# Order of small operations and a later GpSimd scaling in the norm between two attention layers

## The chip, the cores and the metric

The kernel runs on one core of a Trainium2 chip. The metric is the device time of one execution in microseconds. TensorE multiplies, VectorE and ScalarE read its results out of PSUM, GpSimd works on SBUF alone, SyncE (SP) issues the loads and stores.

## The reference, cut to what matters

Eight images of 512 channels by 32 x 32 pixels go through two attention layers. The change lies where the first ends and the second begins:

```python
# layer 0, for each image: x is (512, 1024)
out = w_proj @ a + b_proj                       # a: attention output
out = group_norm(out, gn2_scale, gn2_bias)      # 32 groups of 16 channels
x1  = x + out
# layer 1
qkv = w_qkv @ x1                                # rows of w_qkv normalised
rms = sqrt(mean(qkv ** 2, over channels)) + 1e-4
q, k, v = split(qkv / rms)
attn = softmax(q.T @ k * 512 ** -0.5)          # tokens by tokens, 1024 x 1024, one head
out  = (x1 + w_out @ (attn applied to v)) * 2 ** -0.5
```

## The kernel before

**Precision.** Each float32 matrix is held as two parts of the matmul type, hi (the value rounded) and lo (the rest), and a product is three matmuls: hi·hi, hi·lo, lo·hi. ScalarE writes the hi parts and VectorE the lo parts.

**Order of the work.** A loop runs over the eight images (batches); the code for each engine is a queue written out by hand, and the engines meet at semaphores. Two PSUM tiles of 128 x 1024, `big0` and `big1`, are used in turn by nearly every product; the list `BIG` gives the order. `released(key)` makes TensorE wait until the buffer's previous content (the key two places before in `BIG`) has been read. In the boundary the order is: projection tiles `proj` 0 to 3, Gram tiles `g` 0 to 3, then `y` 0 to 3.

**The boundary.** The 512 channels are four blocks of 128 (k = 0 to 3). Blocks 0 and 1 are normalised together as part c = 0 of the norm, blocks 2 and 3 as part c = 1. Part 1, on which the change bears, goes:

- VectorE: statistics of `proj` 2 and 3 (`out_stats`, L1222 to L1227), means (`gn2_mean`).
- TensorE: `gn2_means(1)`, two small matmuls that average over the channels of a group (L437, L439).
- VectorE: `gn2_dev(1)` squares the deviation of each channel's mean (L1096 to L1098).
- TensorE: `gn2_vars(1)`, two small matmuls that average the variances and the squared deviations (L444, L446).
- VectorE: `gn2_veps(1)` adds epsilon (L1101). GpSimd: `group_rstd` raises to -0.5 (L948). VectorE: `gn2_coefs(1)`, three small operations (L1105 to L1107).
- VectorE: `residual(2)` and `residual(3)` (L1252), which write `XA` = normalised out + x.
- ScalarE: `xc_hi` (L896), the hi part of x1. VectorE: `xc_lo` (L1257), its lo part. For blocks 0 and 1 the parts lie in `ST`, for blocks 2 and 3 in `HH` and `HL`.
- GpSimd: x1 itself in float32 (L1003), into `X`. It is read by `gram_product` and at the very end of layer 1.

**The Gram products.** The mean of the squares of q, k and v needs no product with all of w_qkv: with G = w_qkv^T w_qkv folded to its upper blocks, `from_x1` (L626) makes tile g k = the blocks j = 0 to k of G times x1, six matmuls a block (two halves of 512 columns by three parts). `gram_product(k)` on VectorE (L1263) multiplies that tile by float x1. GpSimd adds the four products (L1010), and TensorE sums them over channels (L668) between y 1 and y 2. y tile k (L626 too, 24 matmuls) needs the buffer of the Gram tile two places before it, so y 0 waits for product 2 and y 1 for product 3.

`x1_block(j)` makes TensorE wait for the lo part of block j. TensorE does what it can without blocks 2 and 3 first: tiles 2 and 3 from blocks 0 and 1, 24 matmuls in all, then block 2 of both tiles, then block 3 of tile 3.

**SP's queue** in this stretch: `W<-d_m` (weights of y) after the last projection tile; the next image into `XA` once all four x1 and all four lo parts are done; `W<-d_u` after the last Gram tile.

Of the kernel before, what the change touches and what calls it, by code (L numbers as in the profile page):

```python
# [20 lines left out]
KB = C // P  # L21
# [63 lines left out]
def build(nc, x, wv_t, wp_t, wqk_t, v_qkv, v_out, wo_t, vecs, consts, out):  # L85
    ctx = ExitStack()
    with ctx:
# [214 lines left out]
        def own_wait(eng):  # L302

            eng.sem_inc(s_waited, 1)
# [117 lines left out]
        def _(pe):  # L422
# [58 lines left out]
            def body(b, last_batch):  # L481
                def released(key):

                    i = big_at(b, key)
                    if i >= 2:
                        kind, k = (BIG_LAST if last_batch else BIG)[i - 2]
                        reader, per = {"v": (s_v_ready, 5), "qk": (s_nat_ready, 16), "s": (s_exp_done, 72),
                                       "proj": (s_pr_ready, 4), "gna": (s_gn_var, GN_PER_BATCH),
                                       "gnb": (s_gn_veps, GN_PER_BATCH),
                                       "g": (s_prod_ready, 4), "r": (s_r_ready, 1),  # L490
                                       "y": (s_y_ready, 4), "u": (s_vp_ready, 8), "s1": (s_s1_ready, 8)}[kind]

                        pe.wait_ge(reader, b * per + k + (GN_PER_BATCH if kind in ("gna", "gnb") else 1))

                    return big[i % 2]
# [108 lines left out]
                def gn2_vars(c):  # L604
                    group_vars(GN_PER_BATCH * b + 2 + c, tps[1][:, 0:2], slice(2 * c, 2 * c + 2), s_gn2_full)
# [15 lines left out]
                def from_x1(t, k, slot, blocks):  # L621
                    for half in range(2):
                        cols = slice(HALF * half, HALF * half + HALF)
                        for j in blocks:
                            for i, (wp, xp) in enumerate(((0, 0), (0, 1), (1, 0))):
                                last = mm(t[:, cols], w_full[slot][:, wp, j, P * k:P * k + P], x1(xp, j)[:, cols],  # L626
                                          start=(j == 0 and i == 0), stop=(j == (k if slot == 0 else KB - 1) and i == 2))
                    return last
# [14 lines left out]
                gn2_means(1)  # L643
                x1_block(1)
                from_x1(t, 1, 0, (1,)).then_inc(s_big_full, 1)
                g2 = released(("g", 2))
                from_x1(g2, 2, 0, (0,))
                gn2_vars(1)
                from_x1(g2, 2, 0, (1,))
                g3 = released(("g", 3))  # L650
                from_x1(g3, 3, 0, (0, 1))
                x1_block(2)
# [281 lines left out]
        @block.gpsimd  # L934
        def _(pool):
            nc.gpsimd.memset(expo[:, 0:8], 0.5)
            nc.gpsimd.memset(expo[:, 8:16], -0.5).then_inc(s_expo_set, 1)
            nc.gpsimd.memset(ones[:], 1.0)
            nc.gpsimd.memset(product_stage(2).bitcast(f32), 0.0).then_inc(s_const_set, 1)
            pool.wait_ge(s_expo_set, 1)  # L940
            for n, rows in ((4, slice(8, 12)), (12, slice(0, 8)), (16, slice(12, 16))):
                pool.wait_ge(s_square_sum, n)
                nc.gpsimd.tensor_tensor(rnorm[:, rows], ssq[:, rows], expo[:, 8:8 + rows.stop - rows.start], ALU.pow)\
                  .then_inc(s_norm_pow, 1)

            def group_rstd(n, rows):
                pool.wait_ge(s_gn_veps, n)
                nc.gpsimd.tensor_tensor(rstd[:, rows], veps[:, rows], expo[:, 8 + rows.start:8 + rows.stop], ALU.pow)\  # L948
                  .then_inc(s_gn_rstd, 1)

            group_rstd(1, slice(0, KB))

            def body(b, last_batch):
                def normalise(n):
                    i = n % 8
                    pool.wait_ge(s_recip_done, b * 72 + n + 1)
                    own_wait(pool)
                    nc.gpsimd.tensor_scalar(PB[:, i, :], PB[:, i, :], rinv[:, i:i + 1], 1.0, ALU.mult, ALU.mult)\  # L958
                      .then_inc(s_p_norm, 1)

                def head_out(u):
                    pool.wait_ge(s_corr_done, b * 16 + u + 1)

                    pool.wait_ge(s_p_norm, b * 72 + min(4 * u + 12, 4 * UNITS0))
                    if u == UNITS0 - 2:
                        pool.wait_ge(s_a_lo, b * 6 + 6)
                    rows, pair, c = slice(64 * (u // 2 % 2), 64 * (u // 2 % 2) + 64), u // 4, u % 2
                    nc.gpsimd.tensor_tensor(XA[rows, pair, HALF * c:HALF * c + HALF], RB[rows, 0:HALF],  # L968
                                            RB[rows, HALF:N], ALU.add).then_inc(s_a_done, 1)
                    pool.wait_ge(s_a_done, b * 16 + u + 1)  # L970
                    own_wait(pool)

                def scale_x(k):
                    if k == 0:
                        pool.wait_ge(s_x_res, b * 16 + 16)
                        own_wait(pool)
                    nc.gpsimd.tensor_scalar(X[:, k, :], X[:, k, :], RES, 1.0, ALU.mult, ALU.mult)\
                      .then_inc(s_x_scaled, 1)

                def a_lo(pair, half):  # L980
                    pool.wait_ge(s_a_hi, b * 8 + 2 * pair + half + 1)
                    cols = slice(HALF * half, HALF * half + HALF)
                    nc.gpsimd.tensor_tensor(HL[:, pair, cols], XA[:, pair, cols], HH[:, pair, cols].bitcast(f32),
                                            ALU.subtract).then_inc(s_a_lo, 1)

                for n in range(4 * UNITS0):
                    normalise(n)
                    if n % 4 == 3 and n >= 8:
                        head_out(n // 4 - 2)
                    if n in X_SCALE_STEPS:  # L990
                        scale_x(X_SCALE_STEPS.index(n))
                    for part in a_parts(n):
                        a_lo(*part)
                head_out(UNITS0 - 2)
                head_out(UNITS0 - 1)
                for c in range(GN2_PARTS):
                    rows = slice(2 * c, 2 * c + 2)
                    group_rstd(GN_PER_BATCH * b + 2 + c, rows)
                    pool.wait_ge(s_coef_b, b * GN2_PARTS + c + 1)
                    for k in (2 * c, 2 * c + 1):  # L1000
                        pool.wait_ge(s_res_sum, b * KB + k + 1)
                        own_wait(pool)
                        nc.gpsimd.tensor_scalar(X[:, k, :], XA[:, k, :], 1.0, coefB[:, k:k + 1], ALU.mult, ALU.add)\  # L1003
                          .then_inc(s_xc_ready, 1)
                for k in range(1, KB):
                    pool.wait_ge(s_prod_ready, b * KB + k + 1)
                    if k > 1:
                        pool.wait_ge(s_prod_add, b * (KB - 2) + k - 1)
                    own_wait(pool)
                    nc.gpsimd.tensor_tensor(PB[:, 4, :], PB[:, 4, :], PB[:, 4 + k, :], ALU.add)\  # L1010
                      .then_inc(s_prod_add if k < KB - 1 else s_prod_sum, 1)
                pool.wait_ge(s_ms_done, b + 1)
                nc.gpsimd.tensor_tensor(rms, mean_sq, expo[:, 0:8], ALU.pow).then_inc(s_rms_done, 1)
                for i in range(8):
                    if i == 4:
                        normalise(64 + 3)
                    pool.wait_ge(s_s1_ready, b * 8 + i + 1)
                    own_wait(pool)
                    nc.gpsimd.tensor_scalar(negmax[:, i:i + 1], rowmax1[:, i:i + 1], rcol[:, i:i + 1], -1.0,  # L1019
                                            ALU.mult, ALU.mult).then_inc(s_neg_ready, 1)  # L1020
                    if i == 7 and not last_batch:
                        group_rstd(GN_PER_BATCH * (b + 1) + 1, slice(0, KB))
                    if i and i != 4:
                        normalise(64 + i - 1)
                normalise(71)

            each_batch(pool, body)
# [3 lines left out]
        def _(dve):  # L1031
# [115 lines left out]
            def body(b, last_batch):  # L1147
# [93 lines left out]
                def gn2_veps(c):  # L1241
                    dve.wait_ge(s_gn2_full, b * 2 * GN2_PARTS + 2 * c + 2)
                    group_veps(tps[1][:, 0:2], slice(2 * c, 2 * c + 2))
# [34 lines left out]
                xc_lo(1)  # L1278
                gram_product(0)
                gn2_dev(1)  # L1280
                gram_product(1)
                gn2_veps(1)
                gn2_coefs(1)
                residual(2)
                residual(3)
# [146 lines left out]
```

## Time and profile before

| | |
|---|---|
| time, median of 3 runs | 3522.6 us (3520.0 to 3522.65) |
| profiled execution | 3520.63 us, span 3518.8 us |
| TensorE busy | 3457.8 us, 98% of the span, 17360 matmuls |
| VectorE busy | 2077.7 us, 59% |
| ScalarE busy | 1826.7 us, 52% |
| GpSimd busy | 1086.0 us, 31% |
| granted TensorE clock, mean | 0.999 of full speed |

Busy time says how long an engine had an instruction in hand. TensorE has one nearly always, so the 2% in which it has none, and the stretches in which its matmuls are slower, are what an order of work can change. One batch takes about 430 us.

### The profile page before, as it was taken

To read this page: it belongs to the slowest core of one execution; us is meant where nothing else is said; L and a number is where in the kernel's file an instruction comes from. 1 tells how busy PE (TensorE), PEld (TensorE's weight loads), DVE (VectorE), ACT (ScalarE), POOL (GpSimd) and SP (SyncE) were. 2 spreads that over 40 slices of the span, in tenths; PEclk is the share of its full clock that TensorE was granted. 3 is DMA by queue.
4 is the path that set the end of the run, shared out by engine and by line. 5 is a ranking of instruction groups with operands and counts; after the bars stand their busy time and mean duration, and the time that the engine had idled before them with its cause. 6 is when DMAs were issued, how large, how long until landed. Compare 5 with 4: busy or idle time off the path is not lost.

```text
span 3518.8 us, 52658 instructions
## 1 busy us (share of the span) xinstructions
PE 3457.8 (98%) x17360; PEld 2832.2 (80%) x17360; DVE 2077.7 (59%) x3388; ACT 1826.7 (52%) x3074; POOL 1086.0 (31%) x947
## 2 busy tenths in 40 slices
PE   7999999999999999999999999999999999999999
PEld 4788888878888788887878878788787887888878
DVE  4677436773378634786347854488444884457742
ACT  3677226862278522784237832388223882247822
POOL 0344203441045410453104531145211452124521
PEclk9999999999999999999999999999999999999999
DMA  8522214312234113331143220342213422142210
GB/s 312 156 53 61 92 54 127 85 37 84 82 99 97 66 43 103 89 86 72 37 121 89 68 84 34 112 97 61 84 37 110 95 61 84 43 137 62 61 48 24
DMA packets 63519, 294.41 MB, mean 84 GB/s; under 512 B 9200, under 2 KB 9456, under 8 KB 52464
## 3 DMA queue, kind: packets, MB, share of 16 engines
q1 hardware_dynamic: 63216, 290.65, 28.0%
q8 instruction: 156, 2.56, 0.3%
q14 instruction: 147, 1.20, 0.1%
HBM read 158.49 MB, written 31.46 MB: 54 GB/s over the span
## 4 chain that ended last, share of the span: by engine, by line
PE 85%; issue 6%; DVE 3%; ACT 2%; DMA 2%; POOL 2%; SPq 0%; ACTq 0%; DVEq 0%; POOLq 0%
PE big L430 28%; PE tps L529 14%; PE big L556 12%; PE ops L542 12%; PE ops L702 10%; PE big L626 6%; PE ops L430 1%; DVE XA L1252 1%; ACT PB L828 1%; PE big L594 1%; DMA d_m<-PT 1%; DMA d_u<-ST 1%; POOL XA L968 1%; DVE HL L1257 0%; DVE small L1180 0%
## 5 line engine op out<-in xcount | busy, mean ns | idle before, releaser
L958 POOL TENSOR_SCALAR PB<-PB,small 128x1024 f32<-128x1024 f32 x576 | 650.2, 1129 | 1304.4 <-DVE small L1186 1293.6
L834 ACT ACTIVATE PT<-tps 128x512 fp32r<-128x512 f32 x1088 | 601.7, 597 | 250.9 <-PE tps L529 247.8
L1191 DVE TENSOR_TENSOR PT<-tps,PT 128x512 fp32r<-128x512 f32 x1088 | 693.8, 679 | 39.0 <-ACT PT L834 38.6
L1180 DVE TENSOR_REDUCE small<-big 128x1 f32<-128x1024 f32 x512 | 625.1, 1221 | 63.7 <-PE big L556 60.3
L529 PEld LDWEIGHTS tps<-ident,PB 128*128 128x128 f32 x4608 | 526.8, 140 | 125.5 <-DVE PT L1191 56.2
L529 PE MATMUL tps<-ident,PB 128*128 128x128 f32 x4608 | 618.0, 275 | 9.0 <-DVE PT L1191 6.1
L828 ACT ACTIVATE PB<-big,small 128x1024 f32<-128x1024 f32 x512 | 572.6, 1118 | 74.3 <-DVE small L1180 71.3
L542 PE MATMUL ops<-PT,VT 128*128 128x512 f32 x2048 | 599.2, 414 | 0.0
L556 PE MATMUL big<-ST 128*128 128x512 f32 x2048 | 555.0, 393 | 12.3 <-ACT PB L828 11.2
L556 PEld LDWEIGHTS big<-ST 128*128 128x128 f32 x2048 | 381.9, 188 | 103.2 <-ACT PB L828 19.8
L542 PEld LDWEIGHTS ops<-PT,VT 128*128 128x128 f32 x2048 | 346.1, 189 | 47.4 <-DVE PT L1191 5.0
L430 PE MATMUL big<-HH,W 128*128 128x512 f32 x1024 | 333.6, 390 | 1.9 <-DVE ST L1054 1.1
L1172 DVE SCALAR_TENSOR_TENSOR ST<-big,vec,ST 128x512 fp32r<-128x512 f32 x128 | 96.1, 751 | 326.7 <-ACT ST L820 326.7
L820 ACT ACTIVATE ST<-big,vec 128x512 fp32r<-128x512 f32 x128 | 88.2, 689 | 303.7 <-PE big L430 303.7
L430 PEld LDWEIGHTS big<-HH,W 128*128 128x128 f32 x1024 | 192.2, 188 | 45.6 <-issue 4.5
L1327 DVE CUSTOM_DVE_ANT_0 PB<-big,RB 128x1024 f32<-128x1024 f32 x64 | 78.4, 1225 | 240.3 <-PE big L430 240.3
L968 POOL TENSOR_TENSOR XA<-RB 64x512 f32<-64x512 f32 x128 | 164.1, 1282 | 142.4 <-ACT RB L845 141.1
L1019 POOL TENSOR_SCALAR small<-small 128x1 f32<-128x1 f32 x64 | 17.1, 267 | 616.7 <-DVE small L1327 607.7
L430 PE MATMUL big<-HL,W 128*128 128x512 f32 x512 | 199.9, 390 | 0.0
L430 PE MATMUL big<-W,HH 128*128 128x512 f32 x640 | 197.2, 389 | 0.0
L702 PE MATMUL ops<-PT,VT 128*128 128x512 f32 x768 | 188.3, 394 | 0.0
L626 PE MATMUL big<-ST,W 128*128 128x512 f32 x720 | 183.1, 395 | 1.2 <-ACT XA L886 1.2
(158 smaller groups left out, 4652.2 us busy)
## 6 DMA issues: line engine op xcount, KB each, us to landing
ST<-ST SPq DMA_DIRECT2D x384, 256.0 KB, 5.0
W<-d_qk SPq DMA_DIRECT2D x32, 1024.0 KB, 5.3
XA<-in_x SPq DMA_DIRECT2D x8, 2048.0 KB, 7.7
X<-in_x SPq DMA_DIRECT2D x8, 2048.0 KB, 10.5
W<-d_wp SPq DMA_DIRECT2D x8, 2048.0 KB, 11.6
W<-d_g SPq DMA_DIRECT2D x8, 2048.0 KB, 11.9
W<-d_m SPq DMA_DIRECT2D x8, 2048.0 KB, 7.9
W<-d_u SPq DMA_DIRECT2D x8, 2048.0 KB, 10.2
```

Of the source, the lines that this page charges most:

```text
L430: last = mm(dst, stat(sp_, k), mov(mp_, k), start=(i == 0), stop=(i == n - 1))
L529: last = nc.tensor.transpose(tps[n % 2][:, P * t:P * t + P], PB[:, 4 * (u % 2) + t, P * s:P * s + P], ident[:])
L542: last = mm(ops[u % 2][:], VT[:, s, P * (u // 2):P * (u // 2) + P], pt_slot(u, s)[:, part, :], start=(s == 0 and part == 0), stop=(s == 7 ...
L556: last = mm(t[:, cols], stack("q", head)[:, tok:tok + P], stack(kind, head)[:, cols], start=(i == 0), stop=(i == 1))
L626: last = mm(t[:, cols], w_full[slot][:, wp, j, P * k:P * k + P], x1(xp, j)[:, cols], start=(j == 0 and i == 0), stop=(j == (k if slot == 0 ...
L702: last = mm(ops[use % 2][:], VT[:, s, col:col + P], ptb[:, pp, :], start=(s == 0 and i == 0), stop=(s == 7 and i == 2))
L828: act_fn(PB[:, i, :], t[:], ACT.Exp, bias=negmax[:, i:i + 1], accum_out=rowsum[:, i:i + 1])\
L834: act_fn(pt_slot(u, s)[:, 0, :], tps[n % 2][:], ACT.Copy).then_inc(s_pt_hi, 1)
L958: nc.gpsimd.tensor_scalar(PB[:, i, :], PB[:, i, :], rinv[:, i:i + 1], 1.0, ALU.mult, ALU.mult)\
L968: nc.gpsimd.tensor_tensor(XA[rows, pair, HALF * c:HALF * c + HALF], RB[rows, 0:HALF], RB[rows, HALF:N], ALU.add).then_inc(s_a_done, 1)
L1180: V.tensor_reduce(negmax[:, i:i + 1], tile(("s", 4 * u + tb))[:], axis=AX.X, op=ALU.max, negate=True).then_inc(s_row_max, 1)
L1191: V.tensor_tensor(pt_slot(u, s)[:, 1, :], tps[n % 2][:], pt_slot(u, s)[:, 0, :].bitcast(f32), ALU.subtract).then_inc(s_pt_ready, 1)
```

## The change

Three edits. The group products of the variances (part 1) are issued on TensorE before Gram tile 2 is begun, not between its blocks 0 and 1. VectorE adds epsilon before Gram product 1, not after it. GpSimd writes float x1 of blocks 2 and 3 only when the lo parts of all four blocks are done.

```diff
@@ TensorE
                 from_x1(t, 1, 0, (1,)).then_inc(s_big_full, 1)
+                gn2_vars(1)
                 g2 = released(("g", 2))
-                from_x1(g2, 2, 0, (0,))
-                gn2_vars(1)
-                from_x1(g2, 2, 0, (1,))
+                from_x1(g2, 2, 0, (0, 1))
                 g3 = released(("g", 3))
@@ GpSimd
                     for k in (2 * c, 2 * c + 1):
                         pool.wait_ge(s_res_sum, b * KB + k + 1)
+                        if c:
+                            pool.wait_ge(s_xc_lo, b * KB + KB)
                         own_wait(pool)
@@ VectorE
                 gn2_dev(1)
+                gn2_veps(1)
                 gram_product(1)
-                gn2_veps(1)
                 gn2_coefs(1)
```

## Rows read from the trace of the kernel before

**Rows 1.** The page's chain that ended last, shares of the span by engine.

```profile
PE 85%; issue 6%; DVE 3%; ACT 2%; DMA 2%; POOL 2%; SPq 0%; ACTq 0%; DVEq 0%; POOLq 0%
```

**Rows 2.** Waits by engine: who waited for whom, us in total, times, longest us.

```profile
PE big L626 <- DVE HL L1257: 14.6, 8, 1.8
```

**Rows 3.** Timeline of batch 0's boundary: start us, us, engine, line, operation, tiles.

```profile
351.75 1.23 DVE L1263 TENSOR_TENSOR PB<-big,X 128x1024 f32<-128x1024 f32 x1 [0.97 <-PE big L626]
...
353.47 0.16 DVE L1101 TENSOR_SCALAR small<-tps 128x2 f32<-128x2 f32 x1 [0.49 <-PE tps L446]
...
353.71 0.70 POOL L948 TENSOR_TENSOR small<-small 128x2 f32<-128x2 f32 x1 [6.84 <-DVE small L1101]
...
354.45 0.16 DVE L1105 TENSOR_TENSOR small<-small,vec 128x2 f32<-128x2 f32 x1 [0.82 <-POOL small L948]
...
354.92 2.48 DVE L1252 SCALAR_TENSOR_TENSOR XA<-XA,small,X 128x1024 f32<-128x1024 f32 x2
...
356.41 4.04 POOL L1003 TENSOR_SCALAR X<-XA,small 128x1024 f32<-128x1024 f32 x2 [1.99 <-DVE XA L1252]
...
357.42 4.10 DVE L1257 SCALAR_TENSOR_TENSOR HL<-XA,small,HH 128x1024 fp32r<-128x1024 f32 x2
...
359.51 0.50 PE L626 MATMUL big<-HH,W 128*128 128x512 f32 x1 [1.83 <-DVE HL L1257]
```

**Rows 4.** The same timeline, TensorE around the stall and the squared deviation.

```profile
350.06 3.03 PE L626 MATMUL big<-ST,W 128*128 128x512 f32 x12
...
350.62 0.15 DVE L1098 TENSOR_TENSOR small<-small 128x2 f32<-128x2 f32 x1
...
353.29 4.38 PE L626 MATMUL big<-ST,W 128*128 128x512 f32 x18
...
363.76 1.52 PE L626 MATMUL big<-ST,W 128*128 128x512 f32 x6
...
374.64 1.84 PE L668 MATMUL ops<-ones,PB 128*128 128x1 f32 x16
```

**Rows 5.** Single lines: count, duration ns min/median/max; then two operations of the timeline.

```profile
L1257 DVE SCALAR_TENSOR_TENSOR ST<-XA,small,ST x16: 1276/1282/1287, 344.6 to 3356.4; 128x1024 fp32r<-128x1024 f32 x16
...
L1257 DVE SCALAR_TENSOR_TENSOR HL<-XA,small,HH x16: 2030/2086/2144, 357.4 to 3367.8; 128x1024 fp32r<-128x1024 f32 x16
...
L1119 DVE TENSOR_TENSOR HL<-XA,HH x32: 1216/1218/1221, 64.8 to 3059.3; 128x1024 fp32r<-128x1024 f32 x32
...
L1003 POOL TENSOR_SCALAR X<-XA,small x32: 1123/1976/2087, 342.2 to 3366.8; 128x1024 f32<-128x1024 f32 x32
...
344.60 1.28 DVE L1257 SCALAR_TENSOR_TENSOR ST<-XA,small,ST 128x1024 fp32r<-128x1024 f32 x1
...
344.90 1.97 POOL L1003 TENSOR_SCALAR X<-XA,small 128x1024 f32<-128x1024 f32 x1 [1.58 <-DVE XA L1252]
```

**Rows 6.** Timeline in the attention, VectorE beside GpSimd; then GpSimd's additions, by line.

```profile
203.97 1.28 DVE L1191 TENSOR_TENSOR PT<-tps,PT 128x512 fp32r<-128x512 f32 x2
...
204.08 1.13 POOL L958 TENSOR_SCALAR PB<-PB,small 128x1024 f32<-128x1024 f32 x1
...
L1010 POOL TENSOR_TENSOR PB<-PB x24: 2387/2400/3368, 360.4 to 3375.4; 128x1024 f32<-128x1024 f32 x24
```

**Rows 7.** The chain in order of time, and one stretch by windows with its granted clock.

```profile
359.51 15.30 PE big L626 x66
...
2508.00 16.87 PE big L626 x66
...
3367.92 16.87 PE big L626 x66
...
2508.00:2512.00 4.00, 4.00 (x11) 3.13 (x12) 3.24 (x2) 0.00 (x0) 4.00 (x2) 0.57 0.17 18
```

**Rows 8.** The load that y needs: its issue in the timeline, and its page row.

```profile
346.79 0.33 SPq L393 DMA_DIRECT2D W<-d_m  x1
...
W<-d_m SPq DMA_DIRECT2D x8, 2048.0 KB, 7.9
```

## The prediction

> **What bounds the kernel now.** I read the page's chain first. TensorE is 85% of what ended last [rows 1], so a change pays only where TensorE stands still or where it starts sooner. Then the waits by engine: in the boundary there is one wait of size, line 626 on VectorE's lo part (line 1257), eight times, once a batch, 14.6 us in all, 1.8 each [rows 2]. The timeline of batch 0 around it shows who is late [rows 3, 4]: TensorE starts 18 matmuls at 353.29, is out of work at 353.29 + 4.38 = 357.67, and starts again at 359.51, 0.05 after the lo part of block 2 has ended (half of the 4.10 us for two, begun at 357.42). Behind the lo part stands a chain on VectorE without a hole: epsilon at 353.47, GpSimd's power of 0.70, the coefficients at 354.45, two residuals of 2.48 in all, lo 2. Without the wait the next matmul would have begun 0.23 after the last one did (0.39 before 357.67), at 357.51. So 2.0 us a batch are there to be had, 16 in eight, and TensorE cannot give back more at this place.
>
> The chain in order of time shows a second loss. The 66 matmuls from this restart take 15.30 us in batch 0, but 16.87 in batches 5 and 7 (counted from 0), where the granted clock falls just behind the wait: 0.57 on average over 2508 to 2512, a mix of 1.2 and 2.4 GHz [rows 7]. That is 1.57 us twice. The other six batches have no such fall.
>
> **The variance product ahead of Gram tile 2.** Moved: six matmuls (block 0 of tile 2) no longer run before the two group products. At 15.30 / 66 = 0.232 each [rows 7] the products, and the epsilon that waits for them, come 6 x 0.232 = 1.39 earlier: 353.47 becomes 352.08. No matmul is added or removed; tile 2's blocks 0 and 1 are issued as one call, in another order of halves. The products read the squared deviation, which VectorE starts at 350.62 and has by 350.77 [rows 4]; they now come at about 351.55, so 0.8 us cover it. If that cover went, TensorE would stand still for the excess. Tile 2 is claimed after the products instead of before; its release, Gram product 0, is ahead of the deviation on VectorE and so is done too.
>
> **Epsilon ahead of Gram product 1.** Before, VectorE ran product 1 at 351.75 to 352.98 and then stood idle until 353.47. After, it runs epsilon (0.16) at 352.08, product 1 (1.23) to about 353.45, and the power on GpSimd (0.70) lies under the product: it is done by 352.08 + 0.16 + 0.08 + 0.70, about 353.05. The coefficients then start at about 353.42 (the records of VectorE overlap by some 0.05) instead of 354.45. Of the 1.39 won, 1.03 arrive; ends of this term: 0.95 if every hand-over costs 0.05, 1.10 if they overlap as the closest pairs do. Product 1 itself ends 0.45 later. It releases the buffer of tile 3, which TensorE claims twelve matmuls after the products, near 354.7: 1.2 us of cover; without it tile 3 would be late by the excess.
>
> **Float x1 behind the lo parts.** This adds a wait on GpSimd for both lo parts before x1 of blocks 2 and 3, and takes nothing away but an overlap. VectorE's lo with float operands in SBUF took 1.28 in sixteen cases and 2.03 to 2.14 in sixteen, and GpSimd's x1 1.12 at best and 1.98 in the median [rows 5]. The timeline reads as turns, not as sharing: the lo begun at 344.60 keeps its 1.28 and the x1 begun at 344.90 takes 1.97, about the rest of the lo plus its own length [rows 5]. At 356.41 x1 2 starts under residual 3, runs when that ends at 357.40, and lo 2 pays for it; x1 3 then makes lo 3 pay [rows 3]. The slow form also differs from the fast one in its tiles (HL and HH, not ST), but the same tiles with two inputs took 1.22 in 32 other operations with GpSimd out of the way [rows 5]. So lo 2 should fall from 2.05 to 1.28, 0.77 won. Its bounds are 0 (the length belongs to the form) and 0.77 (the fast form); I take the upper end, for the 32 rows.
>
> Lo 2 then starts at 357.42 - 1.03 = 356.39 and ends at 357.67, ScalarE's hi part moving with the residual. TensorE restarts at 357.72 instead of 359.51: 1.79 us, with 0.2 of the wait left. By bounds: 1.7 to 2.0.
>
> The Trainium skill speaks against this step in one place. Advanced Engine Details and Errata, VectorE Performance Modes, names only VectorE's two-port mode as what GpSimd and VectorE block each other in, and its table gives that mode to neither form with two tensor inputs. By it lo would stay at 2.05 and the first rival's sum holds. SBUF — State Buffer, "SBUF: two separate sides", counts an operation with two SBUF inputs in, as a lock for a whole instruction; the turns in [rows 5] agree with that page. By it the forecast's sum holds.
>
> **What the delayed x1 holds up.** Queued behind the new wait on GpSimd are x1 2, x1 3, three additions of 2.40 [rows 6] and the power of the norm. Lo 3 ends at 357.67 + 1.28 = 358.95; x1 2 runs 359.00 to 360.13, x1 3 to 361.26 (before: 360.45). Gram product 2 needs x1 2 and runs 360.17 to 361.40. Does it take turns with x1 3? It reads one operand from PSUM; two VectorE operations of that kind ran 1.28 in all beside a GpSimd operation of x1's kind that took 1.13 [rows 6]. I take no delay; the other bound is 1.1 us, the rest of x1 3. Product 2 releases y tile 0. Before, y 0 followed the restart by 363.76 - 359.51 = 4.25 [rows 4], so it is now due at 361.97: 0.57 us of cover. At the other bound the wait would be 0.5 a batch, and the gain 1.3. Product 3 waits for tile 3 as before. The three additions end near 361.3 + 3 x 2.5 = 368.8, and TensorE reads their sum at 374.64 - 1.79 = 372.85 [rows 4]: 4 us of cover.
>
> SP's queue: the next input's load waits for all x1 and all lo; it went when lo 3 ended at 361.52 and now goes when x1 3 does, at 361.26, so it is not later. The load of d_u behind it goes about 1.8 earlier and has the four y tiles of 24 matmuls, 96 x 0.232 = 22 us, before its first use; a load of that size took 7.9 [rows 8], and beside the input's it would take twice that at most. The load that y needs (d_m) was issued at 346.79 and takes about 7.9 [rows 8], so it is there at 354.7, 7 us before 361.97.
>
> **The sum.** 8 x 1.79 = 14.3, and 2 x 1.57 = 3.1 for the halved clock that followed the wait, together 17.4. The profiled execution took 3520.63 (span 3518.8 and 1.8 around it): 3503.2. The median of the three runs is 3522.6, 2.0 above it. My estimate is that these runs had one or two more such falls of the clock (1.57 each), which the change would take away too, so I do not add the 2.0. I forecast 3503.5.
>
> **The rivals.**
> - *Forecast as above*, 0.74. Its own range is 3500.5 (2.0 a batch and no fall) to 3507 (1.7 a batch and both falls).
> - *Lo keeps its 2.05 us*, 0.08. TensorE restarts at 358.46; lo 3 ends at 360.5, product 2 at 362.93, y 0 due at 362.71: 0.22 lost. 0.83 x 8 = 6.6: 3514, or 3511 without the falls. For it: slow lo parts are exactly the ones in HL. Against: the 32 rows at 1.22.
> - *The falls of the clock stay*, 0.08, at this place or another: 14.3 alone, 3506 on the profiled execution, 3508 on the median. For it: six waits of the same length had no fall, so the wait is not enough for one.
> - *No change*, 0.06: the 1.8 us are waited for later in the batch, at a step that TensorE does not set itself. Against: from 359.51 on the chain has nearly only TensorE until the next batch. 3520 to 3525.
> - *Slower*, 0.04: the delayed x1 sets y 0. It decides once product 2 ends after 363.76, 2.4 us later than I have it; x1 2 would need 3.5 us in place of 1.13. To lose 0.2% (7 us) it needs another 0.9 a batch, a product 2 at 364.7: 3530. The most that any GpSimd addition was stretched is 3.37 against 2.40 [rows 6], which is not enough.
>
> About 0.2% is what a measurement of this kernel can tell from no change. Faster by more than that: 0.74 + 0.08 + 0.08 = 0.90; within it 0.06; slower 0.04. The range that leaves out less than 2 in 10 is 3500 to 3511: the forecast's, the clock's rival, and the better half of the first.
>
> **What would show it.** In the profile of the changed kernel: epsilon ahead of product 1 at about 352.1 in batch 0; coefficients near 353.4; all 32 lo parts at 1.28 and x1 2 and 3 at 1.13; the wait of line 626 on line 1257 at 0.2 a batch or gone; no wait of line 626 on line 1263; the span of a batch shorter by 1.8; the 66 matmuls at 15.3 in every batch. The forecast is wrong if the lo in HL stays above 2 us, if a wait of y 0 for product 2 appears, or if a halved clock shows elsewhere.

## The result, and the profile after

The changed kernel takes 3504.56 us (median of 6 runs, 3503.34 to 3505.56); the kernel before, on the same chips, 3522.02 (6 runs, 3519.28 to 3522.65). The ratio is 0.9952, 95% interval 0.9939 to 0.9965: 17.5 us faster. The forecast was 3503.5 in a range of 3500 to 3511. The profiled execution took 3504.55.

The waits of TensorE in the changed kernel (waited in all, times, longest), which answer to [rows 2]:

```profile
PE big L626 <- DVE HL L1258: 3.0, 7, 0.4
...
PE big L626 <- ACT XA L885: 1.1, 7, 0.2
```
The wait on the lo part fell from 14.6 us to 3.0, and from eight times to seven. No wait of line 626 on Gram product (line 1264 now) is in the list.

The timeline of batch 0's boundary, which answers to [rows 3, 4] (this execution reached the boundary about 0.15 us later than the one before; the lo part of block 0, for one, begins at 344.74 and not 344.60):

```profile
352.23 0.16 DVE L1102 TENSOR_SCALAR small<-tps 128x2 f32<-128x2 f32 x1 [1.32 <-PE tps L446]
352.47 0.70 POOL L947 TENSOR_TENSOR small<-small 128x2 f32<-128x2 f32 x1 [5.46 <-DVE small L1102]
352.75 1.23 DVE L1264 TENSOR_TENSOR PB<-big,X 128x1024 f32<-128x1024 f32 x1 [0.36 <-issue]
353.89 0.15 DVE L1106 TENSOR_TENSOR small<-small,vec 128x2 f32<-128x2 f32 x1
...
354.35 2.48 DVE L1253 SCALAR_TENSOR_TENSOR XA<-XA,small,X 128x1024 f32<-128x1024 f32 x2
...
356.86 2.48 DVE L1258 SCALAR_TENSOR_TENSOR HL<-XA,small,HH 128x1024 fp32r<-128x1024 f32 x2
...
358.19 0.50 PE L626 MATMUL big<-HH,W 128*128 128x512 f32 x1 [0.45 <-DVE HL L1258]
...
359.55 2.23 POOL L1004 TENSOR_SCALAR X<-XA,small 128x1024 f32<-128x1024 f32 x2 [6.37 <-DVE HL L1258]
...
360.77 1.23 DVE L1264 TENSOR_TENSOR PB<-big,X 128x1024 f32<-128x1024 f32 x1 [1.43 <-POOL X L1004]
...
362.04 0.41 SPq L398 DMA_DIRECT2D XA<-in_x  x1
...
362.41 1.52 PE L626 MATMUL big<-ST,W 128*128 128x512 f32 x6
```
Read it from top to bottom. Epsilon starts at 352.23, which is 352.08 on the clock of the kernel before, as forecast. Gram product 1 should follow at once, but starts 0.36 after epsilon's end. So the coefficients start at 353.89 (353.74, forecast 353.42) and TensorE at 358.19 (358.04, forecast 357.72), 1.47 earlier than before and not 1.79. Both lo parts are short, 2.48 for the two. x1 2 and 3 follow them, 2.23 for the two, product 2 ends at 362.00, and y 0 starts at 362.41 without a wait.

The same lines as single groups, to be read against [rows 5]:

```profile
L1258 DVE SCALAR_TENSOR_TENSOR ST<-XA,small,ST x16: 1277/1284/1286, 344.7 to 3343.9; 128x1024 fp32r<-128x1024 f32 x16
L1258 DVE SCALAR_TENSOR_TENSOR HL<-XA,small,HH x16: 1277/1282/1286, 356.9 to 3353.4; 128x1024 fp32r<-128x1024 f32 x16
```
```profile
L1004 POOL TENSOR_SCALAR X<-XA,small x32: 1120/1127/1977, 342.3 to 3356.0; 128x1024 f32<-128x1024 f32 x32
```
The lo parts in HL are as short as those in ST, 1.28; the median of the 32 x1 is 1.13 where it was 1.98.

The last batch differs in one thing. In it, whose code is written out behind the loop with constants as thresholds, the product follows epsilon without a gap and TensorE does not wait:

```profile
3347.98 0.16 DVE L1102 TENSOR_SCALAR small<-tps 128x2 f32<-128x2 f32 x1 [1.32 <-PE tps L446]
3348.06 1.23 DVE L1264 TENSOR_TENSOR PB<-big,X 128x1024 f32<-128x1024 f32 x1
...
3349.20 0.15 DVE L1106 TENSOR_TENSOR small<-small,vec 128x2 f32<-128x2 f32 x1
...
3352.16 2.48 DVE L1258 SCALAR_TENSOR_TENSOR HL<-XA,small,HH 128x1024 fp32r<-128x1024 f32 x2
...
3353.50 0.50 PE L626 MATMUL big<-HH,W 128*128 128x512 f32 x1
```
And the chain in order of time has 66 matmuls of the same length behind every restart, which answers to [rows 7]; first and last of the eight:

```profile
358.19 15.26 PE big L626 x66
...
3353.50 15.30 PE big L626 x66
```
All eight lie between 15.25 and 15.30; there is no fall of the clock.

### The profile page after: what moved, and what is told of

It reads as the page before. It is cut to its first block, busy times and chain, and to the rows that moved or that the text cites. A ratio compares the mean times of both kernels' runs of the same rounds, so it can differ in the third digit from the quotient of the medians.

```text
span 3502.8 us, 52659 instructions
## 1 busy us (share of the span) xinstructions
PE 3454.2 (99%) x17360; PEld 2830.5 (81%) x17360; DVE 2064.4 (59%) x3388; ACT 1825.9 (52%) x3074; POOL 1061.2 (30%) x947
## 4 chain that ended last, share of the span: by engine, by line
PE 91%; DVE 2%; ACT 2%; DMA 2%; issue 2%; POOL 0%; SPq 0%; ACTq 0%; DVEq 0%; POOLq 0%
PE big L430 28%; PE tps L529 14%; PE ops L542 13%; PE big L556 12%; PE ops L701 10%; PE big L626 7%; PE big L594 5%; PE ops L430 1%; ACT PB L827 1%; DMA d_m<-PT 1%; DMA d_u<-ST 1%; DVE small L1181 0%; PE big L678 0%; PE ops L667 0%; ACT XA L885 0%
```

## The experiments

Three edits on one kernel can hide each other, so each half was tried alone, then the disputed gap, then the rival on the slower side, then the clock. Medians are of 5 to 11 runs; each ratio is against the kernel before on the same chip. The set-up ahead of batch 0 differs between executions (the lo part of block 0 begins at 342.80 in the profile of the first experiment and at 347.07 in that of epsilon alone, 4.3 us apart), so I also compare within a profile: from TensorE's first restart behind the wait to its eighth (seven batches), less 1.57 for each fall of the clock in between. Before: 3367.92 - 359.51 - 1.57 = 3006.84 by [rows 7], and 3006.21, 3006.16 and 3005.87 in the three repeats at the end of this section, 3006.27 in the mean. Changed: 3353.50 - 358.19 = 2995.31, which is 10.96 / 7 = 1.57 less a batch. (That this is also the cost of a fall is chance.)

**Float x1 alone.** The kernel before with the third edit:

```diff
                         pool.wait_ge(s_res_sum, b * KB + k + 1)
+                        if c:
+                            pool.wait_ge(s_xc_lo, b * KB + KB)
                         own_wait(pool)
```

> The third edit alone, on the kernel before. By the theory of turns (GpSimd's x1 and VectorE's lo, with two float inputs in SBUF, run one after the other) all lo parts take 1.24 to 1.28 us, TensorE restarts 0.8 us earlier a batch, 6.1 us in eight, and the wait of line 626 on the lo part falls from 1.8 to about 1.0; with the halved clock as often as before that is 3516, without it 3513. By the rival (the length of 2.05 belongs to the operation with its tiles in HL) nothing moves: 3522 and a wait of 1.8.

Measured: 3510.33 us, ratio 0.9968 (0.9956 to 0.9980). Its line group and TensorE's waits:

```profile
L1259 DVE SCALAR_TENSOR_TENSOR HL<-XA,small,HH x16: 1276/1282/1287, 355.6 to 3358.0; 128x1024 fp32r<-128x1024 f32 x16
```
```profile
PE big L626 <- DVE HL L1259: 8.6, 8, 1.1
```
All sixteen are short, and the wait went from 1.83 to 1.08. From the first restart to the eighth it is 3358.11 - 356.95 = 3001.16, 0.73 less a batch. The rival that the length belongs to the operation in HL has fallen. The median gained 12.4 (3522.77 before), double what the wait gave, and lies 2.7 below the 3513 that I had for a kernel without falls, which counted only the two falls of the first profile; this profile has no fall of the clock. That difference is taken up below.

**The order alone.** The kernel before with the first two edits (their diff stands above).

> The first two edits alone, no later x1. The coefficients start about 0.7 us earlier in seven batches and 1.0 in the last, lo 2 stays at 2.05: TensorE restarts about 0.7 earlier, 6 us in eight, 3516 with the falls of the clock and 3513 without. If the two halves of the change add up, this and the run of the third edit alone together give 12 us and the whole change the rest by the clock.

Measured: 3510.33 us, ratio 0.9967 (0.9955 to 0.9980). The wait is 1.19 in batch 0, the lo parts are long again:

```profile
353.49 0.15 DVE L1104 TENSOR_TENSOR small<-small,vec 128x2 f32<-128x2 f32 x1
...
355.44 4.04 POOL L1002 TENSOR_SCALAR X<-XA,small 128x1024 f32<-128x1024 f32 x2 [2.66 <-DVE XA L1251]
356.45 4.10 DVE L1256 SCALAR_TENSOR_TENSOR HL<-XA,small,HH 128x1024 fp32r<-128x1024 f32 x2
...
358.54 0.50 PE L626 MATMUL big<-HH,W 128*128 128x512 f32 x1 [1.19 <-DVE HL L1256]
```
First restart to eighth: 3359.14 - 358.54 = 3000.60, 0.81 less a batch. The two halves add up: 0.73 + 0.81 = 1.54 against 1.57 for the whole. By the medians they do not: 12.4 + 12.4 - 17.5 = 7.3 too much. Neither half's profile has a fall of the clock, and what the falls cost can be won only once. The mean granted clock of every run was taken too, to three places: it is 1.000 in all twelve runs of the two halves and 0.997 to 0.999 in the thirteen of the kernel before on that chip, which points the same way. As with x1 alone, the 3513 that I had without falls is 2.7 too high.

**The variance products alone.** The kernel before with the first edit only.

> The first edit alone: the variance products ahead of Gram tile 2, epsilon still behind Gram product 1. VectorE is in the product until 352.98 when the variances come, so epsilon moves from 353.47 to about 353.03 and the power of 0.7 on GpSimd lies open again: 0.45 us a batch, 3.6 in eight, 3518. The rival says that the 1.39 us by which the products are earlier reach the coefficients whole: 3511.

Measured: 3512.03 us, ratio 0.9974 (0.9962 to 0.9985). VectorE in batch 0:

```profile
352.89 1.23 DVE L1262 TENSOR_TENSOR PB<-big,X 128x1024 f32<-128x1024 f32 x1 [0.97 <-PE big L626]
...
354.03 0.15 DVE L1100 TENSOR_SCALAR small<-tps 128x2 f32<-128x2 f32 x1
354.26 0.70 POOL L947 TENSOR_TENSOR small<-small 128x2 f32<-128x2 f32 x1 [6.25 <-DVE small L1100]
355.00 0.16 DVE L1104 TENSOR_TENSOR small<-small,vec 128x2 f32<-128x2 f32 x1 [0.82 <-POOL small L947]
...
360.06 0.50 PE L626 MATMUL big<-HH,W 128*128 128x512 f32 x1 [1.31 <-DVE HL L1256]
```
Epsilon waits for the product's end, and the power lies open, as expected. The coefficients start 2.11 after the product does, where it was 354.45 - 351.75 = 2.70 before [rows 3]: 0.59 won, the wait down by 0.52, 0.62 a batch from first restart to eighth (3361.97 - 360.06 = 3001.91). I had 0.45. The median is near the 3511 that I gave the rival, but the rival's way is not there: the wait of 1.31 is still to be seen. My 3518 counted the falls of the clock as unchanged, and this profile has none behind the wait. Two of the seven runs did lose clock: 3514.55 and 3515.16 at a mean granted clock of 0.998, the other five 3510.32 to 3512.99 at 1.000. In which batch they lost it is not on record.

**Epsilon alone.** The kernel before with the second edit only.

> The second edit alone, on the kernel before: epsilon ahead of Gram product 1 with the variance products still between the blocks of tile 2. Epsilon stays at 353.47, the product starts at about 353.9 (with the gap of 0.36) and ends at 355.1, the coefficients start at 355.1 in place of 354.45: 0.65 us later a batch, a wait of 2.5, 5 us slower, 3527, and more where a longer wait brings more falls of the clock (up to 6 of 1.57). If the edit is harmless by itself, 3522.

Measured: 3524.09 us, ratio 1.0006 (0.9997 to 1.0015).

```profile
355.94 0.16 DVE L1101 TENSOR_SCALAR small<-tps 128x2 f32<-128x2 f32 x1 [2.70 <-PE tps L446]
...
356.46 1.23 DVE L1263 TENSOR_TENSOR PB<-big,X 128x1024 f32<-128x1024 f32 x1 [0.36 <-issue]
357.60 0.15 DVE L1105 TENSOR_TENSOR small<-small,vec 128x2 f32<-128x2 f32 x1
...
357.74 3.01 PE L626 MATMUL big<-ST,W 128*128 128x512 f32 x12 [0.33 <-DVE PB L1263]
...
362.64 0.50 PE L626 MATMUL big<-HH,W 128*128 128x512 f32 x1 [1.90 <-DVE HL L1257]
```
The coefficients start 1.66 after epsilon (0.98 before), and tile 3's claim now costs TensorE 0.33, because product 1 is later by more than its cover. The restarts lie 3372.59 - 362.64 = 3009.95 apart, 0.53 more a batch, so by the waits this edit without the first costs some 4 us. By the median it is 2, within what can be told from no change; I had 5. Its profile shows no fall of the clock although the wait is 1.90, so part of the loss may have been given back there; one profile does not show it. The mean granted clocks point that way: 0.999 in eight of its eleven runs and 1.000 in three, against 0.998 in seven and 0.999 in eight of the fifteen of the kernel before on the same chip.

**The gap of 0.36.** The changed kernel with the waits of product 1 ahead of epsilon:

```diff
+                def gram_waits(k):
+                    dve.wait_ge(s_big_full, at(("g", k)))
+                    dve.wait_ge(s_xc_ready, b * KB + k + 1)
+
                 def gram_product(k):
-                    dve.wait_ge(s_big_full, at(("g", k)))
-                    dve.wait_ge(s_xc_ready, b * KB + k + 1)
+                    if k != 1:
+                        gram_waits(k)
...
                 gn2_dev(1)
+                gram_waits(1)
                 gn2_veps(1)
                 gram_product(1)
```

> The changed kernel with the two waits of Gram product 1 put ahead of the epsilon, nothing else moved. In the changed kernel the product starts 0.36 us after the epsilon has ended, in the seven batches of the loop, and at once in the last batch, whose thresholds are constants. Theory: these 0.36 us are VectorE's queue working out two thresholds in registers, which nothing hides there. Then the product starts 0.08 after the epsilon in every batch, the coefficients and TensorE's restart come 0.3 to 0.4 earlier in seven batches, 2.3 us in all: 3502.3, and the wait of line 626 on the lo part is gone or under 0.1. Rival: the gap comes from GpSimd's power, which begins in it, and stays: 3504.6.

Measured: 3501.29 us (5 runs, 3500.28 to 3501.65), ratio 0.9941 (0.9927 to 0.9954), the fastest kernel of the study.

```profile
351.86 0.16 DVE L1102 TENSOR_SCALAR small<-tps 128x2 f32<-128x2 f32 x1 [1.31 <-PE tps L446]
352.00 1.23 DVE L1268 TENSOR_TENSOR PB<-big,X 128x1024 f32<-128x1024 f32 x1
352.10 0.70 POOL L947 TENSOR_TENSOR small<-small 128x2 f32<-128x2 f32 x1 [5.46 <-DVE small L1102]
353.14 0.15 DVE L1106 TENSOR_TENSOR small<-small,vec 128x2 f32<-128x2 f32 x1
...
356.10 2.48 DVE L1258 SCALAR_TENSOR_TENSOR HL<-XA,small,HH 128x1024 fp32r<-128x1024 f32 x2
...
357.44 0.50 PE L626 MATMUL big<-HH,W 128*128 128x512 f32 x1
```
The product starts at once, and the power still runs under it, so the power was not what held it. TensorE's matmuls no longer wait for the lo part in any batch, and the restarts are 3350.49 - 357.44 = 2993.05 apart, 0.32 less a batch than in the changed kernel. The changed kernel's own trace says what VectorE's queue does there, by line (these are instructions of the queue, not of the engine):

```profile
L1262 DVEq ALU_OP  x28: 40/40/40, 348.2 to 2929.4; - x28
```
```profile
L1263 DVEq EVENT_SEMAPHORE  x32: 21/21/21, 348.3 to 3357.2; - x32
```
28 register operations for four products in seven batches, none in the eighth, beside 32 waits in all eight. The 28 alone are 0.04 each; which operations make up the whole 0.36 this view does not show. That the waits' place makes the gap is shown; how it divides between arithmetic and waits is not.

**The rival on the slower side.** The changed kernel with x1 2 and 3 held back until the last Gram tile is full:

```diff
                         if c:
-                            pool.wait_ge(s_xc_lo, b * KB + KB)
+                            pool.wait_ge(s_big_full, big_count(b, ("g", KB - 1)))
```

> The changed kernel with float x1 of blocks 2 and 3 held back further, until the last Gram tile is full. This is the rival on the slower side, made to happen. x1 2 runs from about 362.8 to 363.9, Gram product 2 ends at 365.2 and y 0, at 362.41 in the changed kernel, starts at about 365.2: 2.8 us a batch, 22 in eight, 3527, plus 1.57 for each fall of the clock that the new wait of some 2.6 us brings. If the cover of y 0 were larger than the timeline says, less than that.

Measured: 3536.78 us, ratio 1.0043 (1.0029 to 1.0056), slower than the kernel before.

```profile
PE big L626 <- DVE PB L1264: 22.5, 8, 2.9
```
```profile
363.49 2.22 POOL L1004 TENSOR_SCALAR X<-XA,small 128x1024 f32<-128x1024 f32 x2 [9.64 <-PE big L626]
364.71 2.36 DVE L1264 TENSOR_TENSOR PB<-big,X 128x1024 f32<-128x1024 f32 x2 [4.71 <-POOL X L1004]
...
366.08 1.63 PE L626 MATMUL big<-ST,W 128*128 128x512 f32 x6 [2.81 <-DVE PB L1264]
```
```profile
797.00:801.00 4.00, 3.73 (x10) 2.92 (x11) 1.26 (x2) 0.00 (x0) 3.83 (x2) 0.59 0.63 194
```
y 0 starts 366.08 - 358.86 = 7.22 after the restart where it was 4.22: 3.0 a batch, 24 in eight. In four of the eight batches the clock fell behind the new wait (the granted clock in the window of batch 1 is 0.59; 48 matmuls took 12.74 to 12.78 there and 11.15 to 11.17 in the other four), 1.6 each. 24 + 6.4 on 3504.6 makes 3535; the other 1.8 are not accounted for, and my 2.8 a batch was 0.2 too small. So the mechanism exists and would turn the result; the change stays on the right side of it by the 0.4 us between 362.00 and 362.41.

**Turns or shares.** The changed kernel with x1 2 behind lo 2 only (`b * KB + KB - 1` in place of `b * KB + KB`).

> The changed kernel with x1 2 waiting for the lo part of block 2 only. By the theory of turns lo 3, which follows lo 2 without a pause, has the first turn and keeps 1.24 to 1.28; the record of x1 2 starts at about 358.4 and is about 2.1 us long, because it stands until lo 3 ends at 359.34 and then runs 1.1; product 2 starts 0.0 to 0.3 earlier, and the time does not change: 3504.6. If the two shared the port by halves, both would be stretched and lo 3 would take over 1.6.

Measured: 3504.52 us, ratio 0.9951 (0.9938 to 0.9965), the changed kernel's time.

```profile
356.05 2.48 DVE L1258 SCALAR_TENSOR_TENSOR HL<-XA,small,HH 128x1024 fp32r<-128x1024 f32 x2
...
357.53 3.10 POOL L1004 TENSOR_SCALAR X<-XA,small 128x1024 f32<-128x1024 f32 x2 [5.16 <-DVE HL L1258]
```
```profile
L1258 DVE SCALAR_TENSOR_TENSOR HL<-XA,small,HH x16: 1276/1282/1286, 356.1 to 3352.4; 128x1024 fp32r<-128x1024 f32 x16
```
x1 2 begins under lo 3 and lo 3 is not stretched (1.29 at most in 16); the pair of x1 takes 3.10 in place of 2.23, 0.87 more, where lo 3 still had 1.0 to run. Turns, then, in the order of arrival, and the operation that arrives second stands for the whole rest.

**How often the clock fell before.** The kernel before three times more, unchanged, for its profile.

> The kernel before once more, for a second profile: how often does the clock fall behind the wait of 1.83 us? The first profile had two falls at 3520.63 and no other difference between batches; the median over the runs is 1.5 to 2 us higher. Theory: the slower runs have one to three falls more, 1.57 each, so the time less 1.57 a fall and less the shift of the first restart against 359.51 is 3517.5 within 0.5. Rival: the spread lies in the set-up ahead of batch 0 alone, and there are two falls again.

> The same kernel, for a third profile, with the same expectation: by the theory the time less 1.57 a fall and less the shift of the first restart is 3517.5 within 0.5, and the number of falls differs from profile to profile; by the rival it is two each time.

> The same kernel, for a fourth profile, with the same expectation. If the falls behind this wait account for the part of the gain that the waits do not (17.5 by the medians, 12 by the waits), the mean over the profiles is three or four falls.

Measured: 3519.76, 3521.86 and 3519.41. The chain of the second one, at its first three restarts:

```profile
358.39 16.87 PE big L626 x66
...
789.59 15.26 PE big L626 x66
...
1219.05 16.86 PE big L626 x66
```
The long ones number three, four and three, so with the first profile 2, 3, 4, 3: twelve in 32 batches, all directly behind the wait of 1.83. They are not spread evenly: the last batch fell in all four profiles, batch 5 (counted from 0) in three, batch 2 in two, batches 0, 1 and 4 once each, batches 3 and 6 never. Every one of the 32 waits is 1.82 or 1.83 long, so its length does not choose the batch; what does, no run here tests. Time less 1.57 a fall and less the shift of the first restart (from 359.51 to 357.77, 358.39 and 357.73) is 3516.8, 3516.7 and 3516.5, and 3517.5 for the first profile. The number differs, as the theory says; the constant is 0.7 to 1.0 below what I gave, outside the 0.5 that I had allowed, so some tenths in the batches between are not covered by it. Nor do the falls alone order the times: 3519.76 has three and 3520.63 two, because the set-up of the first is 1.7 shorter. The first and the eighth restart of the repeats are at 357.77 and 3367.12, 358.39 and 3369.26, 357.73 and 3366.74, with two, three and two falls between them.

## Why the prediction was right

- **The wait on lo 2 as the whole prize**: right. Undone in part (1.08, 1.19, 1.31 left) it gave part, and in the kernel with the waits ahead no matmul of line 626 waits for a lo part any more.
- **1.39 from the six matmuls**: right to 0.01 in batch 0.
- **1.03 of it reaching the coefficients**: this is the term that was mis-sized. It is 0.71 in the seven batches of the loop. I let product 1 follow epsilon by the overlap that VectorE's records show elsewhere, and charged its two waits nothing. Before the change VectorE stood 0.97 us for TensorE in front of this product [rows 3], time enough to work them through; behind epsilon nothing covers them. Cost 0.32 x 7 = 2.3 us, measured as 2995.31 - 2993.05 = 2.3 within the profiles and as 3504.56 - 3501.29 = 3.3 by the medians, which are of two different sets of runs. In the last batch, without the gap, epsilon to coefficients is 1.22 and the wait is gone.
- **0.77 from lo 2**: right. 1.28 in all 32, 0.75 less wait with this edit alone. Where the Trainium skill's two pages part (Advanced Engine Details and Errata, VectorE Performance Modes, against SBUF — State Buffer, "SBUF: two separate sides"), these runs agree with the second: float operations with two inputs in SBUF take turns with GpSimd's, and the product with one input in PSUM does not. It ran from 360.77 beside x1 3, and both kept their lengths (1.23, and 2.23 for the two x1).
- **Cover of y 0**: 0.57 forecast, 0.41 measured. x1 2 starts 0.2 after lo 3's end and not 0.05: the hand-over to GpSimd was too cheap in my count. The input's load went at 362.04, before at 361.76, so 0.13 later on the same clock where I had it no later; nobody waits for it.
- **The clock**: 3.1 for two falls, and one or two more as an estimate. Over four profiles the mean is three, 4.7 us. The changed kernel's profile has none.

The sum, as measured: 12.1 from the waits (1.47 in batch 0, 1.38 to 1.52 in the next six and 1.95 in the last, each read between the 120 projection matmuls at a batch's start and the restart), 4.7 from the clock, together 16.8 of 17.5. The forecast had 14.3 + 3.1 = 17.4. So the mechanism was right, but that the sum agrees to 0.1 is luck: two errors cancel, 2.2 too much for the waits and 1.6 too little for the clock, with 0.7 unassigned. The forecast lies 1.1 low because I took the sum from the profiled 3520.63, 1.4 under the median of 3522.02, and then put the 3503.2 that came out up to 3503.5 without a reason. One bound is added up wrongly: 2.0 a batch and no fall make 3520.63 - 16 - 3.1 = 3501.5, not 3500.5.

Open: why one wait of 1.83 brings a fall and the next does not, and why 1.90 brought none in the one profile of epsilon alone. In the profiles, waits of 1.1 to 1.3 brought none in 24 batches, 1.83 twelve in 32, 2.8 four in eight; yet two of the seven runs with the wait of 1.31 have a lower mean clock (the variance products alone, above), so none in 24 does not mean never. (That mean takes in the set-up as well: the profile of the kernel with the waits ahead reads 0.999 without a fall at the boundary, because 0.91 was granted over 20 to 40 us.) Length seems to count, but does not decide by itself. The falls of the other runs cannot be counted one by one, but their mean granted clocks go with their times: of the 28 runs of the kernel before beside the experiments, the 15 at 0.997 or 0.998 took 3521.5 to 3524.4, and the 13 at 0.999 took 3519.0 to 3522.0. The profile with four falls reads 0.998, those with two and three 0.999, and the four profiled executions average 3520.4, 1.6 under the median. My estimate from these numbers is that a median run had four falls rather than three. Four falls make 12.1 + 6.3 = 18.4 against the measured 17.5, three make 16.8; what the difference is stays open.

## What to carry to other kernels

A stall on the bounding engine is worth more than its length when the clock may fall behind it: count the slow stretches in several profiles and put them in the sum at their mean. When an operation is moved behind a wait that ends late, look at what its own waits cost in the queue; put those that are long satisfied ahead of the late one. Of a helper engine's work that nobody needs yet, ask whose operation it takes turns with: moved behind, it costs only its own cover, and that cover must be worked out.

## What the runs showed of the hardware

- Two waits, for which the queue of VectorE ran register operations (28 of 0.04 us in seven batches), held VectorE for 0.36 us behind an operation that had itself waited; with constant thresholds in the last batch, or ahead of that operation, for nothing that shows.
- GpSimd and VectorE take turns whole: an x1 of 1.12 alone is on record for up to 2.0 when it arrives under a lo part, and the lo part then keeps its 1.28.
- TensorE's granted clock fell to 1.2 GHz in twelve of 32 batches of the kernel before, each time just behind the same wait of 1.83 us, at 1.57 us a fall (0.57 granted over 2508 to 2512, 1.00 over the 4 us before).
